# Two stage seams and a shared wait: where rows are loaded and when GpSimd prepares the bias, in a macaron transformer block

## What is computed

```python
x = L0_attn_resid                                   # (2, 1024, 1024) float32
x = x + 0.5 * ffn(layernorm(x), ...)                # the same weights twice
x = x + attn(layernorm(x), Wq, Wk, Wv, Wo)
x = x + 0.5 * ffn(layernorm(x), ...)

def ffn(x):                                         # 8 experts, top 2, rank 16
    logits = x @ gate_w.T
    w, sel = top_k(logits, 2);  w = softmax(w)
    w_full = sum(one_hot(sel, 8) * w[..., None])
    low = einsum('bsd,erd->ebsr', x, lora_A)
    return x @ base_w.T + base_b + 2.0 * einsum('ebsr,eor,bse->bso', low, lora_B, w_full)
```

## Time and profile before

| | us |
|---|---|
| runs, lowest, median, highest | 1573.46, 1575.81, 1577.57 |
| profiled execution, its time | 1575.4 |
| its span, first to last instruction | 1573.6 |
| TensorE busy | 1524.4 (97%) |
| VectorE busy | 967.3 (61%) |
| ScalarE busy | 587.0 (37%) |
| GpSimd busy | 694.0 (44%) |

### The profile page before, as it was taken

One profiled execution on the slowest core, in us unless ns is written; L12 is line 12 of the kernel. 1 busy time (PEld: TensorE's weight loads), 2 busy tenths in 40 slices (PEclk: granted clock), 3 DMA queues, 4 the chain that ended last, 5 costly groups with the idle time before them and its releaser, 6 DMA issues. The chain is left out here.

```text
span 1573.6 us, 26210 instructions
## 1 busy us (share of the span) xinstructions
PE 1524.4 (97%) x9184; PEld 1191.0 (76%) x9184; DVE 967.3 (61%) x2727; ACT 587.0 (37%) x1185; POOL 694.0 (44%) x414
## 2 busy tenths in 40 slices
PE   7999998999999969999999999999999999999999
PEld 7999998888888845555555555555478999999998
DVE  7545464556473468888888888888655434343433
ACT  4333233211111125666666666666633222121210
POOL 1222222533343415888888888888612101010100
PEclk8999999999999969999999999999999999999999
DMA  6322324342322362344433333441161212121201
GB/s 230 124 109 98 123 96 149 134 135 82 120 94 81 111 133 62 82 98 101 90 81 76 75 82 83 100 103 30 48 224 59 67 55 68 53 73 47 79 16 41
DMA packets 118774, 145.96 MB, mean 93 GB/s; under 512 B 40976, under 2 KB 77072, under 8 KB 118384
## 3 DMA queue, kind: packets, MB, share of 16 engines
q1 hardware_dynamic: 90064, 120.59, 26.5%
q10 hardware_dynamic: 28592, 23.86, 4.6%
HBM read 95.66 MB, written 53.51 MB: 95 GB/s over the span
## 5 line engine op out<-in xcount | busy, mean ns | idle before, releaser
L1504 ACT ACTIVATE at_probs<-ps 128x512 f32<-128x512 f32 (+3 forms) x768 | 324.6, 494 | 151.2 <-PE ps L1413 149.1
L1573 DVE CUSTOM_DVE_ANT_0 ps<-ps,at_score_mask 128x512 f32<-128x512 f32 (+3 forms) x512 | 290.7, 618 | 36.4 <-PE ps L1402 33.4
L329 POOL TENSOR_TENSOR f_x_ring<-f_x_ring,f_half_bias 128x1024 f32<-128x1024 f32 x32 | 77.3, 2416 | 312.8 <-DVE f_h L590 312.3
L1342 POOL TENSOR_TENSOR at_added<-at_added,at_probs 128x2048 f32<-128x2048 f32 (+1 forms) x60 | 211.4, 3523 | 2.1
L1413 PE MATMUL ps<-at_qs,at_ks 98*128 98x512 f32 (+3 forms) x528 | 192.3, 390 | 4.3 <-ACT at_probs L1504 2.9
L1402 PE MATMUL ps<-at_ks,at_qs 96*128 96x512 f32 (+3 forms) x528 | 175.4, 368 | 12.0 <-DMA at_ks<-scr_k_hi 11.3
L1413 PEld LDWEIGHTS ps<-at_qs,at_ks 98*128 98x128 f32 x528 | 97.3, 193 | 110.5 <-ACT at_probs L1504 86.4
L1428 PE MATMUL ps<-at_probs,at_vs 128*32 128x512 f32 (+3 forms) x1536 | 162.8, 496 | 0.0
L1573 DVE CUSTOM_DVE_ANT_0 ps<-ps,at_score_mask,at_part_max 128x128 f32<-128x128 f32 (+3 forms) x256 | 133.2, 556 | 12.8 <-issue 10.4
L48 PE MATMUL f_ps<-f_wt_hi,f_hT_hi 128*128 128x400 f32 (+1 forms) x384 | 134.3, 350 | 3.2 <-DVE f_hT_lo L594 3.2
L48 PE MATMUL ps<-f_wt_hi,f_hT_hi 128*128 128x400 f32 (+1 forms) x384 | 132.1, 344 | 0.0
(11 more groups left out here) (164 smaller groups left out, 3163.4 us busy)
## 6 DMA issues: line engine op xcount, KB each, us to landing
at_qs<-scr_q_hi SPq DMA_DIRECT2D x20, 512.0 KB, 5.9
f_x_ring<-in_L_attn_resid SPq DMA_DIRECT2D x16, 512.0 KB, 3.5
x<-f_x_ring SPq DMA_DIRECT2D x16, 512.0 KB, 2.7
early<-x SPq DMA_DIRECT2D x16, 512.0 KB, 3.3
scr_q_hi<-qkv_rope_hi ACTq DMA_DIRECT2D x32, 256.0 KB, 2.0
scr_q_lo<-qkv_rope_lo ACTq DMA_DIRECT2D x32, 256.0 KB, 2.3
scr_ctx<-at_ctxn SPq DMA_DIRECT2D x32, 256.0 KB, 2.3
shared<-scr_ctx SPq DMA_DIRECT2D x16, 512.0 KB, 4.5
```

What stands on the lines that cost most here:

```text
L329: pool.tensor_tensor(x_ring[:, u, :], x_ring[:, u, :], half_bias[:], ALU.add).then_inc(bias_added, 1)
L1342: pool.tensor_tensor(added[:, heads, :], first, probs[:, u % PROBS, heads, :], ALU.add).then_inc(added_done, 1)
L1504: act.activation(probs[:, u % PROBS, g, 0:z - a], score_ps[(u * G + g) % BANKS][:, 0:z - a], ACT.Exp, scale=SCALE).then_inc(exp_done, 1)
L1573: dve.tensor_tensor_reduce(out=src, in0=src, in1=mask, scale=1.0, scalar=part_max[:, g, own] if c else -3.0e38, op0=ALU.add, op1=ALU.max, ...
```

## The change

The change has three parts.

1. The load of the identity matrix (used by TensorE to turn tiles) is issued from ScalarE's queue at the start of its list, and no longer first in SP's.
2. GpSimd's list in a feed-forward stage: before it halves the bias it waits, in "f2", for the low parts of the second turned tile (`hT_lo_done` 2) in place of all weights. In "f1", the bias addition of tile 0 waits for `low_s` of tile 0 and that of tile 1 for `low_s` of tile 1, and both are placed before the first low part of Wq. The first four tiles are written out; the loop begins with the second four.
3. In the projection stage, SP's wait for the four turns and the loads of the rows of tiles 4 and 5 stand before the fifth piece of the key and value weights. The loop of row loads begins with tile 6.

```diff
             if attn:
                 for loaded in ctx_loaded:
                     sp.sem_inc(loaded, 16)
-            if prep:
-                sp.dma_start(ident[:], consts["identity"]).then_inc(ident_loaded, 16)
             load_x(sp, 0, 0)
...
+            def add_bias(i, u):
+                pool.wait_ge(h_ready, 4 * i + u + 1)
+                pool.tensor_tensor(x_ring[:, u, :], x_ring[:, u, :], half_bias[:], ALU.add).then_inc(bias_added, 1)
+
+            def low_wq(i, u):
+                pool.wait_ge(wq_hi_done, 4 * i + (u + 1))
+                pool.tensor_tensor(wq_piece(1, i, u), wq_raw[:, u % 2, :], wq_piece(0, i, u).bitcast(F32),
+                                   ALU.subtract).then_inc(wq_lo_done, 1)
+
             if attn:
-                pool.wait_ge(w_lo_done, KC + 1)
+                pool.wait_ge(hT_lo_done, 2)
             pool.wait_ge(bias_loaded, 16)
             pool.tensor_scalar(half_bias[:], half_bias[:], 0.5, None, ALU.mult).then_inc(bias_ready, 1)
             pool.wait_ge(bias_ready, 1)
-            with pool.Fori(0, NT // 4, 1) as i:
+            if prep:
+                pool.wait_ge(low_ready, 1)
+            add_bias(0, 0)
+            if prep:
+                pool.wait_ge(low_ready, 2)
+            add_bias(0, 1)
+            for u in range(4):
+                if u >= 2:
+                    add_bias(0, u)
+                if prep:
+                    low_wq(0, u)
+            with pool.Fori(1, NT // 4, 1) as i:
                 for u in range(4):
-
-                    pool.wait_ge(h_ready, 4 * i + u + 1)
-                    pool.tensor_tensor(x_ring[:, u, :], x_ring[:, u, :], half_bias[:], ALU.add).then_inc(bias_added, 1)
+                    add_bias(i, u)
                     if prep:
-                        pool.wait_ge(wq_hi_done, 4 * i + (u + 1))
-                        pool.tensor_tensor(wq_piece(1, i, u), wq_raw[:, u % 2, :], wq_piece(0, i, u).bitcast(F32),
-                                           ALU.subtract).then_inc(wq_lo_done, 1)
+                        low_wq(i, u)
...
+            if prep:
+                act.dma_start(ident[:], consts["identity"]).then_inc(ident_loaded, 16)
             act.wait_ge(eps_set, 1)
...
             for j in range(KC):
+                if j == WRAW:
+                    sp.wait_ge(h_turned, TC + 1)
+                    for slot in range(2):
+                        load_x(TC + slot, slot)
                 if j >= WRAW:
                     sp.wait_ge(wkv_lo_done, j - WRAW + 1)
                 for cols, src in ((slice(0, KV), w["Wk"]), (slice(KV, 2 * KV), w["Wv"])):
                     sp.dma_start(wkv_raw[:, j % WRAW, cols], src[j * P:(j + 1) * P, :]).then_inc(wkv_loaded[j % WRAW], 16)
-            sp.wait_ge(h_turned, TC + 1)
-            with sp.Fori(TC // 2, NT // 2, 1) as i:
+            with sp.Fori(TC // 2 + 1, NT // 2, 1) as i:
                 for slot in range(2):
                     load_x(2 * i + slot, slot)
```

## The result

Five runs of the changed kernel took 1565.27 to 1570.57 us, median 1567.66, beside five of the kernel before with a median of 1575.67: 8.0 us less, ratio 0.995, 95% interval [0.9933, 0.9966]. The forecast was 1564.2 in a range of 1560.5 to 1569.0. The profiled execution took 1565.27 us (span 1563.4), 10.1 less than the profiled execution before.

The account below looks back on a forecast made before the run. TensorE, busy 97%, bounds the kernel; gains come from its idle time and low-clock stretches. 1575.4 less 2.6 (first stage, start included), 4.2 (projection) and 4.4 (second stage) gives 1564.2 us, range 1560.5 to 1569.

Parts of the forecast that it names:

- the three seams: TensorE idles 2.05 us in first feed-forward, 2.87 in projection, 2.70 in second feed-forward; slow clock then costs 1.7, 1.5, 1.7.
- Part 4: Second feed-forward stage: halving waits for tile 1's low parts, the 2.70 us wait goes, clock adds 1.7: 4.4 us (3 to 4.4).
- part 2, first stage: First feed-forward stage: bias additions behind first routings gain 4.5 us, less 1.5 idle at tile 2 and 0.7 for clock.
- part 3: Projection stage: tiles 4 and 5 rows ahead of last weights cut idle and keep the clock: 4.2 us (2.7 to 4.4).
- Part 1: Kernel start: identity on ScalarE's queue lets SP's first row tile issue some 0.4 us earlier: 0.3 us (0 to 0.45).
- idle 0.3 ... I take idle 0.2: Projection seam: square root after last weight conversion starts TensorE at 284.2 against 283.9, so idle falls from 2.87 to 0.2.
- the bound I had named: Projection seam: tile 4's normalization may meet GpSimd's two pieces; behind both it ends 1.4 us later.
- Quiet third tile: First feed-forward stage: Wq piece lands early enough or the new collision is hidden; gain there 5.2, time 1561.6; chance 0.17.
- Weights become the wait: Projection stage: weight pieces behind the rows come 1 to 3 us late; gain about 1, time 1567.4; chance 0.12.
- Second-stage seam replaced: Second feed-forward stage: tile 0's sum or tile 1's parts come late, so no gain there; time 1568.6; chance 0.06.
- doing nothing: Lines 604, 613, 617 were stretched by something else and rows land no sooner; about 1574; chance 0.04.
- The slower rival: Loop: GpSimd's low part and bias meet every routing, up to 2.6 us lost in each of 12 tiles; 1595; chance 0.01.

Follow-up runs that it names:

- e2: Kernel before with only GpSimd's new waits and order in the first feed-forward stage, written out, old wait in the second: 1580.61 us, ratio 1.0014.
- e1: Kernel before with only the identity's load moved to ScalarE's queue: 1580.59 us, ratio 1.0009.
- c3: Changed kernel with tile 4's square root behind the sixth weight conversion, ScalarE's batch loop in that stage written out: 1564.97 us, ratio 0.9923.
- d1: Kernel before with GpSimd's new list in the first feed-forward stage alone, old loop and wait in the second: 1575.12 us, ratio 0.9985.
- c0: The changed kernel again, unedited, beside new runs of the kernel before: 1568.43 us, ratio 0.9944.
- c1: Changed kernel with the identity's load back on SP's queue: 1568.01 us, ratio 0.9942.
- e3: Kernel before with only GpSimd's new wait in the second feed-forward stage, old list: 1574.79 us, ratio 0.9972.
- e4: Kernel before with only the projection stage's row loads of tiles 4 and 5 ahead of the last weights: 1573.69 us, ratio 0.9968.
- c2: Changed kernel with GpSimd's second low part of Wq and tile 2's bias addition behind the third routing: 1567.00 us, ratio 0.9926.
- d0_combined: Changed kernel with the edits of c1, c2 and c3 together: 1561.84 us, ratio 0.9897.

## Why the prediction came out as it did

The forecast's own case came out: the three seams were removed by the mechanism that it named, and the time lies in its range. The three terms of the seams, named as in the prediction (its Part 4 is the second stage's half of part 2 of the change), against the sections of the 14 profiles, each averaged over the kernels with and without the part. Left out are the kernels with a further edit in that section, e2 in the last row among them:

| term | forecast | sections without | with | difference |
|---|---|---|---|---|
| part 2, first stage | 2.3 | 247.39 (4) | 245.35 (6) | 2.0 |
| part 3 | 4.2 | 298.09 (5) | 293.46 (5) | 4.6 |
| part 4 | 4.4 | 387.48 (4) | 383.03 (9) | 4.45 |

**Part 1, 0.3.** The step "ScalarE issues one DMA ahead of its table load ... this costs nothing" looked at the queue's time alone. Not mentioned: the identity, 2.2 us later, is what TensorE's warm-up waits for. Three comparisons of medians (ScalarE's queue less SP's: +1.1, +0.4 and -0.2) leave it at zero within about 1 us. On the Trainium skill's rule (DMA: Bandwidth & Descriptors, "Issuing engines are not separate DMA queues"), that DMAs from different engines run on the same 16 engines and interleave, the trace agrees: the identity's 128 packets start between 1.8 and 2.3 us in the profile before and between 2.7 and 4.3 in e1, among the packets of the rows and weights. It is the identity that was held up behind the rows, not the rows behind it as I had feared.

**Part 2.** The idle time of 2.05 went to 0.16 (forecast 0.3), and its slow stretch with it. The 1.08 before tile 3's turns went whole. The collision at the third tile came as worked out: idle 1.55, forecast 1.85. In the profile the clock stayed up. So the terms gave 3.4 in the first profile pair (247.74 to 244.31) instead of 2.3: 0.7 for the chance of a fall that did not happen, 0.3 for the collision, and 0.1 for tile 0. The cause that the forecast named, how long tile 0's store takes to free its place, is borne out by the six profiles with this list. Where SP's next load followed the store's issue after 3.3 us (the profile after, c3, d1), TensorE stood still 1.55 to 1.59 us; where it followed after 4.5 (e2, c0, c1), 2.31 to 2.57. The forecast had 1.0 for 2.7 us and 2.7 for 4.8, and took the middle. The even chance of a fall was too high: the clock fell in one of the six, c1, with a section of 247.08. That the average is still 2.0, near 2.3, is partly luck: the idle time for tile 2 averaged 2.0, that for tile 0 0.5 (up to 1.20 in d1), and without this list e3 stood still only 1.53 us for tile 0 and kept its clock.

**Part 3.** Forecast: idle 2.87 to 0.2. Measured in the profile pair: 2.87 to 1.31, and in c0 1.23. The step that failed is "idle 0.3 ... I take idle 0.2". The square root came 0.65 us later in the stage than worked out, because the last weights came later, and normalization took 1.48 instead of 0.82. The second was the bound I had named; here it counts for as much as the first. With TensorE running out of work 0.33 us later than worked out, that leaves 1.1 us off in this profile. By my own list this wait, over 1 us before line 853, was a sign of being wrong.

The rows that now go first did not make the weights late; the clock at the stage's start did. In the profile after it was low for the first 5.3 us of the stage (2.9 before), the turns of the first four tiles took 6.25 us instead of 5.07, and ScalarE, which has to convert those tiles first, began the weights 1.1 us later in the stage (7.22 against 6.09). Over all 14 profiles the last conversion starts 16.10 to 16.52 us into the stage in the five whose turns took 6 us or more (clock low for 4.7 to 5.9 us), with or without part 3, and 15.32 to 16.15 in the other nine: 15.66 on average in the three without part 3, 15.81 in the six with it. And the held-up normalization is not in every execution: in the five profiles with part 3 and the old place of the square root it took 1.48 and 1.77 us (profile after, c0: idle 1.31 and 1.23) or 0.81 to 0.85 (e4, c1, c2: idle 0.48, 0 and 0.46). Where the prediction says that the longest stretch in my rows is 2.24, I misread them: line 606 took 2.32, which is still about one addition.

That the average gain still comes out at 4.6 is partly luck, for a reason that I could not see: the seam's idle time before was 2.87 in the profile that I read, but 4.5 to 4.9 in the four later ones without part 3. The profile before was the mildest case of that wait.

**Part 4.** Right in size and mechanism. From the turn of tile 1 to the low turn of tile 0, 8.17 became 5.32 in the trace (2.85, forecast 2.70), and the stretch behind it, 11.46 us long, became 9.88 (1.58, forecast 1.7). All nine profiles with the new wait agree within 0.1 us.

**What the sum left out.** Attention. The change doesn't touch it, yet it took 624.07 us instead of 622.62 in the profile after, and 622.5 to 629.0 over all 14. In the eight profiles of the changed kernel and its variants it averages 624.5, in the six others 624.9. So it is not the change's doing. It is mostly TensorE's clock behind the wait of 11 us at attention's start: in the first 200 us of attention it was low for 26.6 to 29 us in the nine profiles with 622.5 to 624.5 us, and for 35 to 44 us in the five with 625.9 to 629.0. In the stretch of 34 us below, c2_third_tile (first row) was granted 0.52 and d0_combined (second row) 0.70:

```profile
556.00:590.00 34.00, 31.32 (x117) 18.12 (x117) 25.32 (x90) 8.39 (x19) 5.95 (x5) 0.52 0.36 74
```
```profile
556.00:590.00 34.00, 28.77 (x128) 18.20 (x127) 29.84 (x112) 8.72 (x20) 5.98 (x5) 0.70 0.35 75
```

The profile after cost 1.45 us there against the profile before. The sum for that pair: start 0.6, first stage 3.4, projection 3.1, attention -1.45, second stage 4.5, together 10.2, which is the difference of the spans. Of the 3.5 us between my 1564.2 and the median of 1567.66, then, 1.1 lies in that profile (1565.27), and 2.4 between it and the median: it was the fastest of the five. My step "its time is 0.4 below the median ... which changes nothing here" treated a profile as typical in both kernels. That can't be known from one.

**The rivals.** Quiet third tile: no, the collision is there (1.55, and c2 takes it away). Weights become the wait: the last pieces did come later in that profile, but not because of the rows (see part 3), and the gain was kept. Second-stage seam replaced, and doing nothing: refuted by e3. The slower rival, a collision in every tile of the loop: from tile 2's low turn to the projection stage 206.2 us before (60.27 to 266.44) and 206.2 after (56.17 to 262.38), so nothing.

**Open.** The profiles' averages give 11.1 us for the three terms; the medians of the changed kernel give 8.0 and 9.5, and 11.1 is just beyond both intervals (0.9933 is 10.6 us, 0.993 is 11.0). The runs of single parts show the same gap: by their ratios d1, e3 and e4 gave 2.4, 4.4 and 5.1 us, together 11.9, and the changed kernel 7.9 and 8.8. I know of no cause for the rest beyond scatter, and no run shows one.

## What to carry to other kernels

A seam's price is its idle time and the slow stretch behind it: here 2.7 us of waiting was worth 4.4. When helper work of one engine is moved away from another engine's small steps, work out where it lands next, and check the other users of the same instruction list: writing a loop out moved the additions by 0.16 us and cost 3 us in another stage. Where single runs scatter by as much as the effect, cut the traces at the same instructions and compare the sections; one profile can show a wait at its mildest. And where a load comes late behind a reordering, look at what ran before it, the clock too, in kernels with and without that reordering, before the order is blamed.

## What was not expected of the hardware

- **Which of VectorE's steps GpSimd holds up.** Beside one addition of 2.39 us, the conversion of two numbers took 2.33. Beside the halving of 2.78 us, in e2_bias_first, line 620 took 0.75, line 622 its usual 0.17 and line 629 1.02. The Trainium skill (SBUF — State Buffer, "SBUF: two separate sides") describes an exclusive lock, kept by whichever starts first for its whole instruction; of VectorE's operations it names those in a two-port mode and those with two SBUF inputs. For the additions the trace agrees. Against the halving it doesn't: line 628, with two SBUF inputs, ran in 0.16 us during it, and line 620, also with two, ended after 0.75, with 1.7 us of the halving to go. Between two additions that directly follow each other a pending step got in: lines 631 and 633 of e2_bias_first waited for one addition each, not for both.
- **The clock after a short wait.** Idle time of 1.5 to 1.6 us (in four profiles) was not followed by slow products. Idle of 2.05 to 2.55 was followed by them in the kernel before, e1, e4 and, for tile 2, in c1_identity_back (first row below). Idle of 2.31 in c0_changed (second row) and of 2.57 in e2_bias_first was not:

```profile
59.30:63.50 4.20, 4.20 (x17) 4.17 (x18) 2.94 (x7) 3.15 (x5) 0.71 (x1) 0.66 0.00 0
```
```profile
56.60:60.00 3.40, 3.40 (x19) 3.40 (x20) 2.23 (x6) 2.44 (x5) 0.00 (x1) 1.00 0.00 0
```

- **A small DMA on a second queue.** 64 KB took 4.0 to 4.6 us from issue to landing on ScalarE's queue (six profiles), 1.8 to 2.0 in front of the rows on SP's (eight).
